# Gate logits turned round in a float32 transformer block: the gate's weights stationary, the rows moving

## The reference

```
x = x + 0.5 * ffn(layernorm(x));  x = x + attn(layernorm(x));  x = x + 0.5 * ffn(layernorm(x))

ffn(x):  scores = sigmoid(x @ gate_W) * route_scale            # gate_W is 256 x 8
         top 2 of the 8 scores, divided by their sum, are the gates
         sum over 8 experts of gate * (gelu(x @ W1[e] + b1[e]) @ W2[e] + b2[e])
         + gelu(x @ Ws1 + bs1) @ Ws2 + bs2                      # the shared expert
attn(x): q, k, v with a layernorm each; 16 heads of 64; softmax; Wo; residual; MLP with gelu
```

## Time and profile before

| | |
|---|---|
| median of 3 runs | 2484.05 us (2483.66 to 2486.16) |
| profiled execution, its own time | 2480.43 us |
| its span | 2478.6 us |
| PE busy | 2415.1 us, 97% of the span |
| DVE, ACT, POOL busy | 76%, 67%, 61% |
| first mixture layer, second mixture layer | about 0 to 300 us, about 2221 to 2479 us |

### The profile page before, as it was taken

How to read it: one execution, slowest core, us unless ns; L and a number is a source line. 1 busy time by engine, 2 the same in 40 slices (tenths; PEclk the granted TensorE clock), 3 DMA queues, 4 the chain that set the end, 5 groups by cost and what they waited for, 6 DMA issues and landing times.

```text
span 2478.6 us, 46572 instructions
## 1 busy us (share of the span) xinstructions
PE 2415.1 (97%) x14544; PEld 2097.6 (85%) x14544; DVE 1893.6 (76%) x3626; ACT 1664.7 (67%) x2879; POOL 1505.0 (61%) x1525
## 2 busy tenths in 40 slices
PE   7999979999999999999999999999999999989999
PEld 7888868888888888888888888888888879988888
DVE  4777667878888787887878878788887877766665
ACT  2455567878787787877878778787777853433333
POOL 1233277777776878777787777777768754342211
PEclk9999999999999999999999999999999999999999
DMA  3522432213222122321213212132221354431111
GB/s 134 230 102 87 168 99 73 94 43 98 72 76 94 43 85 72 89 94 43 85 60 93 89 47 93 43 97 72 76 94 43 113 178 152 138 104 35 51 51 43
DMA packets 128038, 220.15 MB, mean 89 GB/s; under 512 B 6922, under 2 KB 89764, under 8 KB 119076
## 3 DMA queue, kind: packets, MB, share of 16 engines
q1 hardware_dynamic: 127908, 218.78, 27.4%
HBM read 114.95 MB, written 53.48 MB: 68 GB/s over the span
## 4 chain that ended last, share of the span: by engine, by line
PE 81%; DVE 8%; issue 6%; POOL 2%; ACT 2%; DMA 1%; SPq 0%; DVEq 0%; ACTq 0%; POOLq 0%
PE a_ov L1529 19%; PE a_sc L1493 18%; PE a_tr L1505 18%; PE a_pj L1448 7%; PE a_pj L1457 4%; PE g_acc L856 3%; PE g_hid L819 3%; PE f_hid L819 2%; PE f_acc L856 2%; PE m_proj L1920 1%; PE f_gbc L898 1%; PE m_acc L1957 1%; DVE f_hp L656 1%; PE m_hid L1986 1%; DVE g_hp L656 1%
## 5 line engine op out<-in xcount | busy, mean ns | idle before, releaser
L1410 DVE TENSOR_REDUCE a_nmax<-a_sc 128x1 f32<-128x1024 f32 x512 | 626.6, 1224 | 259.3 <-PE a_sc L1493 251.0
L1335 POOL TENSOR_SCALAR a_pr<-a_pr,a_rden 128x1024 f32<-128x1024 f32 x512 | 578.1, 1130 | 257.5 <-DVE a_rden L1415 186.5
L1256 ACT ACTIVATE a_pT<-a_tr 128x512 fp32r<-128x512 f32 x1024 | 560.1, 596 | 208.7 <-PE a_tr L1505 202.7
L1421 DVE TENSOR_TENSOR a_pT<-a_tr,a_pT 128x512 fp32r<-128x512 f32 x1024 | 649.4, 676 | 17.5 <-ACT a_pT L1256 17.5
L1529 PE MATMUL a_ov<-a_pT,a_v_s 128*128 128x512 f32 x2048 | 600.5, 415 | 3.2 <-DVE a_half L1401 2.0
L1262 ACT ACTIVATE a_pr<-a_sc,a_nmax 128x1024 f32<-128x1024 f32 x512 | 574.0, 1121 | 32.6 <-DVE a_nmax L1410 29.5
L1493 PE MATMUL a_sc<-a_k_s,a_q_s 128*128 128x512 f32 x2048 | 555.5, 393 | 7.8 <-DMA a_k_s<-a_k_s 7.5
L1505 PEld LDWEIGHTS a_tr<-f_ident,a_pr 128*128 128x128 f32 x4096 | 473.8, 140 | 92.2 <-DVE a_pT L1421 18.5
L1505 PE MATMUL a_tr<-f_ident,a_pr 128*128 128x128 f32 x4096 | 537.6, 273 | 9.2 <-DVE a_pT L1421 9.1
L1493 PEld LDWEIGHTS a_sc<-a_k_s,a_q_s 128*128 128x128 f32 x2048 | 381.0, 189 | 89.0 <-DMA a_k_s<-a_k_s 7.7
L1529 PEld LDWEIGHTS a_ov<-a_pT,a_v_s 128*128 128x128 f32 x2048 | 347.5, 189 | 54.4 <-issue 5.0
(11 more groups left out here) (207 smaller groups left out, 3281.7 us busy)
## 6 DMA issues: line engine op xcount, KB each, us to landing
a_z_s<-zT SPq DMA_DIRECT2D x32, 1024.0 KB, 7.7
a_k_s<-a_k_s SPq DMA_DIRECT2D x64, 512.0 KB, 5.6
a_wqk_s<-w_split SPq DMA_DIRECT2D x64, 256.0 KB, 3.1
a_v_s<-a_v_b SPq DMA_DIRECT2D x16, 1024.0 KB, 4.6
att<-a_ao SPq DMA_DIRECT2D x32, 512.0 KB, 2.9
m_in<-att SPq DMA_DIRECT2D x16, 1024.0 KB, 6.0
a_wv_s<-w_split SPq DMA_DIRECT2D x17, 512.0 KB, 3.8
zT<-f_zT SPq DMA_DIRECT2D x8, 1024.0 KB, 3.9
```

Of the source, the lines that this page charges most:

```text
L1256: act.activation(pT[:, (u // 4) % 2, 0, 4 * part:4 * part + 4, (u % 4) * P:(u % 4 + 1) * P], tr[:, part].rearrange("p (t q) -> p t q", t=4 ...
L1335: pool.tensor_scalar(pr[:, k % NP], pr[:, k % NP], rden[:, k % NP:k % NP + 1], 1.0, ALU.mult, ALU.mult).then_inc(s["normed"], 1)
L1410: dve.tensor_reduce(nmax[:, k % NP:k % NP + 1], sc[:, k % 2], AX.X, ALU.max, negate=True).then_inc(s["negmax"], 1)
L1421: dve.tensor_tensor(to[:, 1], tr[:, part].rearrange("p (t q) -> p t q", t=4), to[:, 0].bitcast(F32), ALU.subtract).then_inc(s["tr_lo"], 1)
```

## The change

The logits are computed the other way round. The gate's weights (16 or 8 columns) are stationary and the 512 transposed rows move: four matmuls that give the logits transposed, 16 partitions by 512, in `aux[:, 0]`. ACT copies these into a new SBUF tile `lgT` (`logits_out`, e = 4, after the high part of slot 3). PE transposes the four tiles of `lgT` back into `aux[:, 1]` (`logits_up`, after the second layer in e = 4). `neg_logits` reads from there, and is moved on DVE from e = 4 to e = 5. `lgT` is zeroed once by POOL in each layer. In the step before the second layer, `logits_out` stands after `hT_hi(7)` on ACT and `logits_up` between the second and the third first-layer product of the MLP on PE.

```
 def logits(i, par):                                    # PE, e = 3
     pe.wait_ge(s["xT_lo"], i * DC + DC)
-    for t in range(NT):
-        for c in range(DC):
-            for k in range(2):
-                n = 2 * E if k == 0 else E
-                o = pe.matmul(aux[:, 0, t * 2 * E:t * 2 * E + n],
-                              xT[:, par, c, k, t * P:(t + 1) * P],
-                              gwp[:, c].rearrange("p k e -> p (k e)")[:, 0:n], ...)
+    for c in range(DC):
+        for k in range(2):
+            n = 2 * E if k == 0 else E
+            o = pe.matmul(aux[0:n, 0], gwp[:, c].rearrange("p k e -> p (k e)")[:, 0:n], xT[:, par, c, k], ...)
+    o.then_inc(s["lgT_ps"], 1)
+
+def logits_up(i):                                      # PE, e = 4
+    pe.wait_ge(s["lgT"], i + 1)
+    for t in range(NT):
+        o = pe.transpose(aux[:, 1, t * P:(t + 1) * P], lgT[:, t * P:(t + 1) * P], ident[:])
     o.then_inc(s["logits"], 1)

+def logits_out(i):                                     # ACT, e = 4
+    act.wait_ge(s["lgT_ps"], i + 1)
+    if isinstance(i, int) and i == 0:
+        act.wait_ge(s["padded"], 1)
+    act.activation(lgT[0:2 * E], aux[0:2 * E, 0], ACT.Identity).then_inc(s["lgT"], 1)

 # ACT body
+    if e == 4 and not last:
+        logits_out(i + 1)
     if e == 4 and tail and not first:
         z_norm(i - 1)
 # PE body
     if e == 3:
         logits(i + 1, 1 - par)
+    if e == 4:
+        logits_up(i + 1)
 # DVE body
-    if e == 4:
+    if e == 5:
         neg_logits(i + 1)
     ...
     if e == 5:
         zz_stats(i - 1)
 # POOL pad()
+    pool.memset(lgT[:], 0.0)
     pool.memset(gpad[:], 0.0).then_inc(s["padded"], 1)
 # last steps of the stage before: ACT, after hT_hi(7); PE, inside the loop over hc
+    ahead["logits_out"]()
+    if isinstance(i, int) and i == NB - 1 and hc == 2: ahead["logits_up"]()
```

More of the change, by code:

```diff
@@ L177, in ffn_phase @@
         xres = m.sb("xres", [P, NT, D], room=rooms.rows)
+        lgT = m.sb("lgT", [P, BT], room=rooms.rows)
         res = m.sb("res", [P, NT, D], room=rooms.tail)
@@ L204, in ffn_phase @@
         gpad = m.sb("gpad", [P, NT, P], room=rooms.tail)
+        lgT = m.sb("lgT", [P, BT], room=rooms.tail)
         xin = m.sb("xin", [P, 2, NT, D], room=rooms.xin)
@@ L231, in ffn_phase @@
     aux = m.ps("aux", [P, 2, BT], AUX_BANK)
-    names = ("veps x_in xres bn stats rstd xn xT_ps xT_hi xT_lo logits neg expneg "
+    names = ("veps x_in xres bn stats rstd xn xT_ps xT_hi xT_lo lgT_ps lgT logits neg expneg "
              "gate gpad gT_ps gst hid gelu gbc gated h_hi h_lo out res res_out padded")
@@ L480, in on_scalar @@
             xt_hi(0, 0)
+            logits_out(0)
             act.wait_ge(s["w1_in"], 48)
@@ L487, in on_scalar @@
         else:
-            whole.mlp["scalar"](act, dict(xt_hi=lambda: xt_hi(0, 0)))
+            whole.mlp["scalar"](act, dict(xt_hi=lambda: xt_hi(0, 0), logits_out=lambda: logits_out(0)))
             act.preload_act_table(ACT.Gelu)
@@ L584, in neg_logits @@
         def neg_logits(i):
-            ps = aux[:, 0, 0:NT * 2 * E].rearrange("p (t k e) -> p t k e", t=NT, k=2)
+            ps = aux[:, 1].rearrange("p (t x) -> p t x", t=NT)[:, :, 0:2 * E].rearrange("p t (k e) -> p t k e", k=2)
             dve.wait_ge(s["logits"], i + 1)
@@ L791, in logits @@
             pe.wait_ge(s["xT_lo"], i * DC + DC)
-            for t in range(NT):
-                for c in range(DC):
-                    for k in range(2):
-                        n = 2 * E if k == 0 else E
-                        o = pe.matmul(aux[:, 0, t * 2 * E:t * 2 * E + n],
-                                      xT[:, par, c, k, t * P:(t + 1) * P],
-                                      gwp[:, c].rearrange("p k e -> p (k e)")[:, 0:n],
-                                      start=(t == 0 and c == 0 and k == 0), stop=(c == DC - 1 and k == 1),
-                                      skip_group_check=True)
+            for c in range(DC):
+                for k in range(2):
+                    n = 2 * E if k == 0 else E
+                    o = pe.matmul(aux[0:n, 0], gwp[:, c].rearrange("p k e -> p (k e)")[:, 0:n], xT[:, par, c, k],
+                                  start=(c == 0 and k == 0), stop=(c == DC - 1 and k == 1), skip_group_check=True)
+            o.then_inc(s["lgT_ps"], 1)
+        def logits_up(i):
+            pe.wait_ge(s["lgT"], i + 1)
+            for t in range(NT):
+                o = pe.transpose(aux[:, 1, t * P:(t + 1) * P], lgT[:, t * P:(t + 1) * P], ident[:])
             o.then_inc(s["logits"], 1)
@@ L892, in on_tensor @@
             logits(0, 0)
+            logits_up(0)
             pe.wait_ge(s["qkv_in"], 80)
@@ L903, in on_tensor @@
         else:
-            whole.mlp["tensor"](pe, dict(transposes=lambda: transposes(0, xn, s["xn"], s["xT_ps"]), logits=lambda: logits(0, 0)))
+            whole.mlp["tensor"](pe, dict(transposes=lambda: transposes(0, xn, s["xn"], s["xT_ps"]), logits=lambda: logits(0, 0),
+                                         logits_up=lambda: logits_up(0)))
             pe.wait_ge(s["w1_back"], 32)
@@ L1760, in body @@
                 hT_hi(i)
+            if isinstance(i, int) and i == NB - 1:
+                ahead["logits_out"]()
             if has(i, 2):
@@ L1979, in body @@
                 for hc in range(HC):
+                    if isinstance(i, int) and i == NB - 1 and hc == 2:
+                        ahead["logits_up"]()
                     if hc >= 2 or has(i, -1):
```

## The result

| | before | after |
|---|---|---|
| median | 2485.11 us (4 runs, 2483.66 to 2488.87) | 2501.82 us (4 runs, 2500.88 to 2503.00) |
| ratio | | 1.0069, 95% interval 1.0056 to 1.0083 |
| profiled execution | 2480.43 us | 2500.93 us |
| its span | 2478.6 us | 2499.1 us |

The changed kernel is 0.7% slower. The forecast was 2502 us, with a range of 2494 to 2512.

What follows compares the result with a forecast made beforehand. PE was taken to bound the kernel (81% of the ending chain), its saving spent on waits. Six first-layer blocks losing 3.0 us each gave +18, on 2484.05 a median of 2502 us; range 2494 to 2512 for 8 in 10.

Steps and rivals of the forecast that it cites:

- step 1: First layer, ACT: `z_norm` stays at 125.11 us, with gelu of slot 5 behind it still at 127.10.
- step 2: First layer: `neg_logits` stands behind DVE's low part, so POOL's `expneg` starts at 129.6 instead of 125.95, 3.6 us later.
- step 3: POOL, first layer: second `z_rstds` is queued behind `expneg`, which ends at 135.0, and ends 2.2 us after its start, at 137.3.
- step 4: ACT stands at `zn_norm` until 137.4 instead of 133.73, 3.7 us later; PE waits for z transposes until 139.5.
- step 5: First layer, DVE's chain to PE: `gates_up` at 144.35 instead of 141.13, the block 3.2 us longer.
- the hand-over: Passage to the second layer: logits 0.8 us shorter, transposes give 0.4 back; put at nothing, 1 us either side.
- the cover of `choices`: Second layer: later `expneg` ends at 2311.9, 0.2 us before `choices` asks; cost nothing, else `choices` waits and holds back gating.
- The turned logits on PE: Per block: 1.71 us of matmuls removed, 0.92 and 0.40 of transposes added; 0.39 less work, spent by a 0.3 wait.
- filling again: PE after its wait for ACT's copy, before the transposes of `logits_up`: restart taken at about 0.1 us.
- only PE's work counts: Rival, whole kernel: work falls 5.5 us and nothing waits, so 2478.5 us; chance 5%.
- the delay absorbed: Rival, first layer: later `expneg` is absorbed, each block loses under 0.8 us, time 2484 to 2489 us; chance 7%.
- The third, the clock: Rival: the clock falls as well, making the kernel slower still than forecast; chance 13%.

Runs made afterwards that it cites:

- the sixth experiment: Changed kernel with `neg_logits` back in slot 4 in the first layer only, still slot 5 in the second: 2483.41 us, ratio 0.9999.
- the fifth experiment: Turned logits, `neg_logits` in slot 4, copy ahead of gelu, plus POOL's hand-over add waiting for DVE's last low part: 2477.99 us, ratio 0.9967 to before.
- the second experiment: Kernel before with one edit, `neg_logits` moved from slot 4 to slot 5, old logits kept: 2500.15 us, ratio 1.0065.
- the first experiment: Changed kernel with `neg_logits` back in slot 4 of DVE, all else as changed: 2484.40 us, ratio 0.9998 to before.
- The third: Changed kernel with `neg_logits` back in slot 4 and ACT's `logits_out` moved ahead of slot 4's gelu: 2479.51 us, ratio 0.9984 to before.
- the fourth experiment: Changed kernel with POOL's order turned, second `z_rstds` ahead of `expneg`: 2517.19 us, ratio 1.0132 to before.

## Why the prediction was right

**Step by step in the first layer.** `z_norm` and gelu stayed in place as forecast (step 1). `expneg` starts 4.47 us after `z_norm`; forecast 4.5 (step 2). `z_rstds` runs directly behind it (step 3). ACT idles 3.04 us before `zn_norm`, forecast some 3.5, and PE 1.80 before the z transposes, forecast 2.4 (step 4). PE waits 0.83 before `gates_up`, forecast about 1 (step 5). `z_norm` to `gates_up` takes 218.17 - 199.34 = 18.83 us, forecast 19.2.

**The size per block was somewhat too large.** In the last four of the six blocks the distance between `gates_up` rows is 34.8 to 35.1, under the forecast's 35.3 to 35.7: five of the six blocks have +2.4 to +2.6 instead of +3.0. The mis-sized term is `z_rstds` in step 3, taken at 2.2 from before (131.47 to 133.69). Behind the later `expneg` it takes 1.88 (209.32 to 211.20). The difference is its second small operation on POOL (L515 before, L527 after), which takes 0.23 us where it took 0.57 in the block of before; there it began 0.20 us behind a low part of DVE (at 131.53), which was not tried as the cause. From `zn_norm` to `gates_up` the chain is as forecast, 218.17 - 211.24 = 6.93 for 6.95. The part of the block ahead of `z_norm` is unchanged, 16.0 to 16.5 us in both kernels (18.0 and 18.1 in block 1).

**The sum came right in part by luck.** The first layer has +17.2 us where +18 was forecast. It is made of 0.4 that the first `gates_up` came later (from 43.0 to 44.3 us over all nine kernels, so no part of the change), 0.8 in block 0, which the forecast had at nothing, and 16.0 in the six blocks: five of about 2.5 and 3.4 in a block where the clock fell. With the hand-over, missed by 3.5, the two profiled spans differ by 20.5 us, 2.5 more than the forecast's 18; the medians differ by 16.7, 1.3 less. That the median of 2501.82 meets the forecast's 2502 to 0.2 us is luck. The mechanism and the size of the first layer's loss are not. The 0.8 of block 0 shows in POOL's and DVE's timeline of the changed kernel:

```profile
63.33 6.44 POOL L543 TENSOR_TENSOR f_nl<-f_ebase,f_nl 128x32 f32<-128x32 f32 x1 [14.28 <-DVE f_nl L602]
```

```profile
69.80 0.18 DVE L619 TENSOR_SCALAR f_sg<-f_nl 128x32 f32<-128x32 f32 x1 [0.78 <-POOL f_nl L543]
```

Here `expneg` takes 6.44 us instead of 5.43. A 1.28 us operation of DVE had started 0.13 us ahead of it. `choices` has to wait 0.78 for `expneg`. There is no z chain in this block; it is the price that the forecast named if the cover of `choices` were gone. The second layer's cover held (the sixth experiment).

**The hand-over was missed.** It was put at nothing with 1 us either way, and costs 3.5. The forecast looked at SP's queue and the w2 load there, and not at what runs on POOL beside DVE's last low part. The wait that it read the earlier trace rows is that of the second `m_acc` piece of the hand-over (2213.62), and this stayed at 2.62 us. The one that grew stands 19 us earlier (2194.99) and was not in its rows. About 2.15 of the 3.5 us is the standstill; the fifth experiment shows the collision as the cause of these. The rest is that the `m_acc` products behind it took 7.51 instead of 6.03 us, at a granted clock of 0.77 instead of 1.00. Whether the longer wait makes that is open. In all six kernels with the 4.77 us wait this piece takes 7.4 to 8.6 us; of the three with 2.62 two take 6.0, but the second experiment's takes 7.52 at a clock of 0.77. Why the turned logits move POOL's add onto the low part is only partly plain. Measured from the start of the pair of low parts, the add starts at 2194.43 - 2193.64 = 0.79 us before and at 2211.81 - 2211.26 = 0.55 after, and the second low part is due at about 0.65, half of the undisturbed 1.29. So a shift of 0.24 us puts the add ahead of it. The shift is there already when POOL's work in this place begins, on the load of `m_xin`: from SP's issue to that start it is 5.19 us before (2184.25 to 2189.44) and 4.93 after (2201.87 to 2206.80). The issue itself takes 1.44 us before and in the second experiment, and 0.51 in all seven kernels with the turned logits. Why it is shorter there, and that it makes the shift, was not tried.

**The turned logits on PE.** Four matmuls with 16 columns stationary take 195.49 - 194.56 = 0.93 us, forecast 0.92. That is 233 ns each, beside 230 with 128 columns stationary (1.38 / 6). The copy of 16 partitions by 512 takes 0.57 (198.18), forecast 0.6; 128 by 512 takes 0.62 just before it (197.66). PE waits 0.27 us for it (198.80 less 198.53, which is the start of the twelve products, 197.10, and the 1.43 that they take in the next slot, 200.92 to 202.35), forecast 0.3. The forecast's 0.1 for filling again after this wait was an estimate that no run shows: the transposes start 0.05 us after the copy's end (198.75 to 198.80) and take 199.21 - 198.80 = 0.41, forecast 0.40. From the logits to the first layer of slot 5 it is 199.21 - 194.56 = 4.65 us; before it was 124.91 - 120.07 = 4.84. So the saving is 0.19 in this stretch, not quite 0. Over the whole block it is less: the first experiment, which has the turned logits alone, is 0.09 a block below before. The third gets 0.3 more.

**The rivals.** That only PE's work counts is refuted by the second experiment: the late `neg_logits` alone costs 15.9 us. Nor is the delay absorbed, with about +2.5 a block where that rival had under 0.8. The third, the clock, came true in one block of six, the one of 35.95 us; from 142 to 149 us the granted clock is 0.76. PE's timeline of the changed kernel there:

```profile
142.97 1.60 PE L798 MATMUL f_aux<-f_ident,f_zn 128*128 128x128 f32 x8 [1.89 <-ACT f_zn L401]
```

The eight transposes take 1.60 us instead of 1.07. From `z_norm` to `gates_up` this block takes 19.44 us where the one above takes 18.83, so the clock costs about 0.6 us. Over the whole layer it is 0.99. The forecast's range took in a few dips of the clock above, and no run shows the size that it gave them; the changed kernel and the second experiment showed one dip each, of about 0.6 us. The second experiment has its 35.94 us block in the same place, with the same clock of 0.76 from 142 to 149; why only this block is hit stays open.

**What stays open.** The profiles put after 20.5 us above before, the medians 16.7. By the table of stages six of the other seven kernels also stand 2 to 5 us higher against before, outside the attention stage, than their medians do. So the one profiled execution of before was a good one. A candidate is the 1.5 us of clock in the hand-over, which this execution of before did not lose (granted clock 1.00) and that of the second experiment did (0.77); then part of the hand-over's 3.5 us is chance. One trace of before can't settle it.

## What to carry to other kernels

Before moving a small operation by a slot, follow it to the longest operation that waits for it, and look at what is queued behind that one: here 0.4 us of DVE work moved by one slot delayed 5.4 us of POOL work, with the path's next link behind it. An engine that is 60% busy can still be late every time. When the long operation can't go behind its successor either, because it has a deadline of its own (the fourth experiment), the remedies are to start it earlier or to make it shorter.

A saving on the bounding engine that is paid with a round trip through another engine is worth only what the round trip leaves: 0.39 us a block less work gave 0.09, until the copy was put where ACT was idle, which gave the rest.

And where DVE and POOL both run wide operations, write down which of DVE's operations each of POOL's will meet. A shift of 0.24 us decided whether 2.15 us fell on the path.

## What the runs showed of the hardware

POOL's add of 128x1024 stopped DVE for 2.1 us in each of the three kernels whose rows are shown, only under different instructions: in the kernel before and in the fifth experiment `g_xn` took 3.46 us and the pair of low parts 1.29, in the changed kernel `g_xn` took 1.37 and the pair 3.44. In these two kernels the instruction that was held came after the add's start (`g_xn` at 2194.85 after 2194.43; the second low part, due at about 2211.9, after 2211.81). POOL's power operation did not hold DVE as the add did. In block 0 the two orders stand side by side, first DVE of the changed kernel, whose `expneg` followed at 63.33 and took 6.44 us, then POOL and DVE of the kernel before:

```profile
63.20 1.28 DVE L692 SCALAR_TENSOR_TENSOR f_qkv_s<-f_qkv_in,f_ln,f_qkv_s 128x1024 fp32r<-128x1024 f32 x1
```

```profile
59.96 5.43 POOL L531 TENSOR_TENSOR f_nl<-f_ebase,f_nl 128x32 f32<-128x32 f32 x1 [11.34 <-DVE f_nl L590]
```

```profile
62.87 1.28 DVE L680 SCALAR_TENSOR_TENSOR f_qkv_s<-f_qkv_in,f_ln,f_qkv_s 128x1024 fp32r<-128x1024 f32 x1 [0.27 <-ACT f_qkv_s L421]
```

Before, the DVE operation ran in the midst of `expneg`, and neither got longer (1.28 and 5.43 us). So did the low part at 128.49, in its usual 0.68 us. Where `expneg` took 6.44, it was the one that started second, 0.13 us behind DVE.

In the fourth experiment, where PE has a wait of 3.13 to 3.23 us in each of the blocks 1 to 6, the granted clock was 1.00 from 50 to 100 us, ahead of the first of these waits, and then 0.94, 0.90 and 0.96 over stretches of 77, 15 and 95 us. In the changed kernel, with waits of 1.80 to 1.89 before the z transposes and 0.75 to 0.83 before `gates_up` (none in the block at 0.76), it was 0.99 over the first layer. The six products at 188.62 of the fourth experiment take 2.91 us, at a granted clock of 0.50 from 188.62 to 191.50; the six at 199.21 of the changed kernel take 1.64, at 1.00.
